# The shared expert's weights and five of its up products moved into the last heads of the first attention

## The reference, cut to what matters

```python
xn = _layernorm(x, axis=-1)
x = x + _L0_attn_ref(xn, Wq, Wk, Wv, Wo) + _L0_ffn_ref(xn, Wg, Wu, Wd, W1, W2)
# in _L0_ffn_ref, xt = xn as (4096, 256):
    h = _gelu(jnp.einsum('td,edf->tef', xt, Wu))      # routed experts, top 2 of 8
    moe = jnp.einsum('ted,te->td', jnp.einsum('tef,efd->ted', h, Wd), cw)
    shared = _gelu(xt @ W1) @ W2                      # W1: 256 x 512, W2: 512 x 256
    return shared + moe
```

## Time and profile before

| | |
|---|---|
| three timed runs | 1799.65, 1786.23, 1797.02 us (median 1797.02) |
| the profiled execution | 1787.63 us, of which the span from first to last instruction is 1785.9 us |
| busy in the span | PE 91%, PE weight loads 68%, DVE 48%, ACT 38%, POOL 42% |
| the chain that ended last | PE 78%, DVE 12%, nothing that the profile shows 4%, ACT 2%, POOL 2%, DMA 1% |
| mean granted clock of PE | 0.955 of 2.4 GHz |

### The profile page before, as it was taken

How to read it: one execution, slowest core, us unless ns; L and a number is a source line. 1 busy time by engine, 2 the same in 40 slices (tenths; PEclk the granted TensorE clock), 3 DMA queues, 4 the chain that set the end, 5 groups by cost and what they waited for, 6 DMA issues and landing times.

```text
span 1785.9 us, 32079 instructions
## 1 busy us (share of the span) xinstructions
PE 1624.5 (91%) x10912; PEld 1212.2 (68%) x10912; DVE 864.5 (48%) x2460; ACT 677.6 (38%) x1680; POOL 741.4 (42%) x845
## 2 busy tenths in 40 slices
PE   6888879898978999999987679998999999999997
PEld 3444434454434899999654346666899999999996
DVE  6787776676721233333164898987322122222221
ACT  4444434454551122222353234432533333333332
POOL 3122234556530255555532248886133333333332
PEclk9799989899988999999998799999999999999999
DMA  8444243345205122222532255544622222222221
GB/s 246 95 124 94 64 92 63 88 75 106 57 4 224 34 72 72 72 71 71 161 111 67 98 171 106 105 88 111 228 37 36 37 37 38 37 38 38 37 36 21
DMA packets 80027, 149.99 MB, mean 84 GB/s; under 512 B 13220, under 2 KB 61472, under 8 KB 73920
## 3 DMA queue, kind: packets, MB, share of 16 engines
q1 hardware_dynamic: 55328, 110.56, 24.1%
q0 software_dynamic: 24544, 37.38, 9.8%
HBM read 103.05 MB, written 44.45 MB: 83 GB/s over the span
## 4 chain that ended last, share of the span: by engine, by line
PE 78%; DVE 12%; issue 4%; ACT 2%; POOL 2%; DMA 1%; DVEq 0%; SPq 0%; ACTq 0%; POOLq 0%
PE PS L1458 21%; PE PS L1476 21%; PE PS L1344 5%; DVE PS L1765 4%; PE PS L1571 3%; PE PS L1423 3%; PE PS L1432 2%; PE PS L1280 2%; PE PS L1662 2%; PE PS L1308 2%; PE PS L1329 2%; PE PS L1443 2%; PE PS L1370 2%; PE PS L1290 2%; PE PS L1581 1%
## 5 line engine op out<-in xcount | busy, mean ns | idle before, releaser
L1458 PEld LDWEIGHTS PS<-arena 128*128 128x128 f32 x3408 | 399.5, 193 | 15.8 <-DVE arena L1988 4.6
L1458 PE MATMUL PS<-arena 128*128 128x128 f32 x3408 | 406.4, 276 | 3.2 <-DVE arena L1988 3.2
L1476 PE MATMUL PS<-arena 128*128 x1704 | 392.3, 379 | 0.0
L1476 PEld LDWEIGHTS PS<-arena 128*128 128x128 f32 x1704 | 311.6, 190 | 40.2 <-issue 0.2
L1988 DVE COPY arena<-PS 128x256 f32<-128x256 f32 x142 | 60.2, 424 | 414.4 <-PE PS L1443 404.0
L1765 DVE CUSTOM_DVE_ANT_0 PS<-PS,arena 128x512 f32<-128x512 f32 (+3 forms) x512 | 234.0, 523 | 31.6 <-PE PS L1308 31.3
L881 POOL DMA_INDIRECT out<-arena x71 | 111.6, 1572 | 314.0 <-ACT arena L1130 293.2
L1120 ACT ACTIVATE arena<-PS,arena 128x128 f32<-128x128 f32 x568 | 161.8, 368 | 138.0 <-PE PS L1458 137.9
L1057 ACT ACTIVATE arena<-PS 128x512 f32<-128x512 f32 (+1 forms) x256 | 167.2, 705 | 74.1 <-PE PS L1329 71.7
L821 POOL TENSOR_SCALAR_AFFINE_SELECT arena<-arena 128x256 f32<-128x256 f32 x256 | 98.2, 409 | 233.0 <-ACT arena L1057 231.8
L867 POOL DMA_INDIRECT arena<-XN,arena x142 | 141.5, 997 | 120.0 <-PE PS L1443 80.9
(11 more groups left out here) (242 smaller groups left out, 2059.7 us busy)
## 6 DMA issues: line engine op xcount, KB each, us to landing
arena<-FD SPq DMA_DIRECT2D x32, 512.0 KB
arena<-in_w SPq DMA_DIRECT2D x16, 1024.0 KB
SPL<-arena SPq DMA_DIRECT2D x32, 384.0 KB, 2.6
arena<-SPL SPq DMA_DIRECT2D x30, 384.0 KB
XN<-arena SPq DMA_DIRECT2D x16, 512.0 KB, 3.2
arena<-SUM SPq DMA_DIRECT2D x16, 512.0 KB, 4.9
arena<-SPL SPq DMA_DIRECT2D x30, 256.0 KB
arena<-SPL SPq DMA_DIRECT2D x34, 128.0 KB, 4.1
```

Source lines behind the costliest of these rows:

```text
L1458: ins = pe.matmul(o, m.now[i % 2][:, c * F + 128 * f:c * F + 128 * f + 128], m.xt[i % 2][:, 128 * c:128 * c + 128], start=(c == 0), stop=( ...
L1476: ins = pe.matmul(to, m.hT[i % len(m.hT)][:, 128 * c:128 * c + 128], m.WD[:, bass.ds(e * (nf * 256) + c * 256, 256)], start=(c == 0), stop ...
```

## The change

The tiles W1 and W2 move to the place of PT (the splits), and are loaded as soon as the last group's splits have been written out, 24 heads before the end. `hs[0]` moves into a pair of STK buffers that the last groups don't use, WD0 behind it. The bias tables are staged over WQ and WK, six heads earlier. Five up products enter plan0: (0,0) before head 120's `scoresT`, (0,1) and (0,2) before the last two `values`, (0,3) after the last `scale`, (1,0) between the two halves of the last `output`. For batch 0 each of the four has a bank of its own (0 to 3), which the scores have left. Their Gelus stand after the last head's Exp. PE and ACT no longer wait for the attention's end before the shared expert, and PE's two waits for banks stand behind it.

```diff
@@ attention_order
         if idx % 8 == 0 and 3 <= idx // 8 + 2 < NHB:
             out.append(("stack", idx // 8 + 2))
-        if idx == NH - 6:
+            if idx // 8 + 2 == NHB - 1:
+                out.append(("shared_weights",))
+        if idx == NH - 12:
             out.append(("bias_rows",))
+        if idx == NH - 8:
+            out.append(("shared_up", 0, 0))
+        if idx == NH:
+            out += [("shared_gelu", 0, fc) for fc in range(3)]
...
             gq = idx // 4 - 1
+            if gq >= 2 * NHB - 2:
+                out.append(("shared_up", 0, gq - 2 * NHB + 3))
             out.append(("values", gq // 2, gq % 2))
...
     while waiting:
         step()
+        if out[-1] == ("scale", NHB - 1, 1):
+            out += [("shared_up", 0, 3), ("shared_gelu", 0, 3)]
+        elif ("unscaleT", NHB - 1) in out[-2:] and ("shared_up", 1, 0) not in out:
+            out += [("shared_up", 1, 0), ("shared_gelu", 1, 0)]
@@ build, the tiles
-        bstage = view(stk_end - 1280, 256)
+        bstage = view(base, 256)
...
-        WD0 = view(base + 8192, 8192)
-        top[0] = LIMIT - 11776
-        W1 = view(carve(1024), 1024).rearrange("p (c n) -> p c n", c=2)
-        W2 = view(carve(1024), 1024).rearrange("p (c n) -> p c n", c=4)
-        hs = [view(carve(2048), 2048).rearrange("p (c n) -> p c n", c=4) for _ in range(2)]
+        hs_at = base + 10240
+        WD0 = view(hs_at + 2048, 8192)
+        W1 = view(pt_at, 1024).rearrange("p (c n) -> p c n", c=2)
+        W2 = view(pt_at + 1024, 1024).rearrange("p (c n) -> p c n", c=4)
+        top[0] = LIMIT - 7680
+        hs = [view(at, 2048).rearrange("p (c n) -> p c n", c=4) for at in (hs_at, carve(2048))]
@@ sync
             def bias_rows():
-                sp.wait_ge(st_made, 16 * (NHB - 1))
+                sp.wait_ge(qk_made, 2 * NHB)
...
+                elif kind == "shared_weights":
+                    for m in range(2):
+                        sp.wait_ge(spl_out[(NHB - 1) % 3][m], 16 * ((NHB - 1) // 3 + 1))
+                    sp.dma_start(W1[:, :, :], t["W1"]).then_inc(w12_in, 16)
+                    sp.dma_start(W2[:, :, :], t["W2"]).then_inc(w12_in, 16)
...
-            attention_over(sp)
-            sp.dma_start(W1[:, :, :], t["W1"]).then_inc(w12_in, 16)
-            sp.dma_start(W2[:, :, :], t["W2"]).then_inc(w12_in, 16)
-            for q in range(4):
-                sp.dma_start(WU0[:, 2048 * q:2048 * q + 2048], t["Wu"][:, 2048 * q:2048 * q + 2048]).then_inc(wu_in, 16)
             sp.wait_ge(b_cut, 5)
             sp.wait_ge(b_set, 1)
             for k in range(3):
                 sp.dma_start(B2S[8 * k:8 * k + 8, :], b3[0:8, k, :]).then_inc(b_rows, 16)
+            attention_over(sp)
+            sp.wait_ge(b_rows, 48)
+            sp.wait_ge(b1_turned, 1)
+            for q in range(4):
+                sp.dma_start(WU0[:, 2048 * q:2048 * q + 2048], t["Wu"][:, 2048 * q:2048 * q + 2048]).then_inc(wu_in, 16)
@@ scalar
+            for b in range(1, HB):
+                for fc in range(1 if b == 1 else 0, 4):
+                    shared_up(b, fc)
             attention_over(act)
-            for b in range(HB):
-                for fc in range(4):
-                    shared_up(b, fc)
@@ tensor
+            def shared_up(b, fc):
+
+                bk = fc if b == 0 else fc % 2
+                if b == 0 and fc == 0:
+                    pe.wait_ge(w12_in, 32)
+                    pe.wait_ge(s_max, 4 * NH)
+                elif b == 0 and fc == 3:
+                    pe.wait_ge(p_made, 2 * NH)
+                elif b:
+                    pe.wait_ge(sh_gelu, 4 * b + fc - 1)
...
+            for b in range(1, HB):
+                for fc in range(1 if b == 1 else 0, 4):
+                    shared_up(b, fc)
+                for i in range(4):
+                    shared_down(b - 1, i)
+            for i in range(4):
+                shared_down(HB - 1, i)
 
             pe.wait_ge(bank[un_last[0]], un_last[1] + 1)
             pe.wait_ge(bank[wo_in_bank[0]], wo_in_bank[1] + 1)
-            pe.wait_ge(w12_in, 32)
...
```

More of the change, by code:

```diff
@@ L341, in build @@
         R16 = [view(carve(16), 16) for _ in range(2)]
+        pt_at = top[0]
         PT = [view(carve(768), 768, BF16).rearrange("p (k s) -> p k s", k=3) for _ in range(2)]
@@ L354, in build @@
         WST = [view(pb0 + 512 * n, 512) for n in range(2)]
-        bstage = view(stk_end - 1280, 256)
-        b3 = view(stk_end - 1024, 3 * 128, BF16).rearrange("p (k n) -> p k n", k=3)
-        b1row = view(stk_end - 512, 128)
+        bstage = view(base, 256)
+        b3 = view(base + 256, 3 * 128, BF16).rearrange("p (k n) -> p k n", k=3)
+        b1row = view(base + 640, 128)
         tiles4 = lambda v: v.rearrange("p (i d) -> p i d", i=4)
@@ L368, in build @@
         WU0 = view(base, 8192)
-        WD0 = view(base + 8192, 8192)
-        top[0] = LIMIT - 11776
-        W1 = view(carve(1024), 1024).rearrange("p (c n) -> p c n", c=2)
-        W2 = view(carve(1024), 1024).rearrange("p (c n) -> p c n", c=4)
-        hs = [view(carve(2048), 2048).rearrange("p (c n) -> p c n", c=4) for _ in range(2)]
+        hs_at = base + 10240
+        WD0 = view(hs_at + 2048, 8192)
+        assert stk_end - 8192 == hs_at and hs_at + 2048 + 8192 <= pt_at
+        W1 = view(pt_at, 1024).rearrange("p (c n) -> p c n", c=2)
+        W2 = view(pt_at + 1024, 1024).rearrange("p (c n) -> p c n", c=4)
+        top[0] = LIMIT - 7680
+        hs = [view(at, 2048).rearrange("p (c n) -> p c n", c=4) for at in (hs_at, carve(2048))]
         moe0_at = top[0]
@@ L1070, in unscaleT @@
                 act.activation(OTT[n % 2][:, :], ps(bk, 0, 512), ACT.Copy).then_inc(bank[bk])
+            def shared_up(b, fc):
+                act.wait_ge(sh_made, 4 * b + fc + 1)
+                if b >= 2:
+                    act.wait_ge(sh_down, 4 * b - 4)
+                act.activation(hs[b % 2][:, fc, :], ps(fc if b == 0 else fc % 2, 0, 512), ACT.Gelu).then_inc(sh_gelu)
             for kind, *a in plan0:
@@ L1090, in scalar @@
                     values(*a)
+                elif kind == "shared_gelu":
+                    shared_up(*a)
                 elif kind == "unscaleT":
@@ L1095, in scalar @@
                     act.activation(RR[0].A, RR[0].A, ACT.Exp).then_inc(r_exp)
[L1097 to L1101, removed]
             def expert_up(layer, i):
@@ L1385, in slots, with shared_up @@
                 ins.then_inc(slot_turned)
+            def shared_up(b, fc):
+                bk = fc if b == 0 else fc % 2
[6 more added lines that the diff above has]
+                    pe.wait_ge(sh_gelu, 4 * b + fc - 1)
+                for c in range(2):
+                    ins = pe.matmul(ps(bk, 0, 512), W1[:, c, 128 * fc:128 * fc + 128], xnT[:, c, 512 * b:512 * b + 512], start=(c == 0), stop=(c == 1))
+                ins.then_inc(sh_made)
             for kind, *a in plan0:
@@ L1397, in tensor @@
                     project_v(*a)
+                elif kind == "shared_up":
+                    shared_up(*a)
                 elif kind == "scores":
@@ L1416, in tensor @@
                     slots(0, 5)
[L1418 to L1424, removed]
             def shared_down(b, i):
@@ L1490, in experts @@
                         expert_down(layer, j)
+            for b in range(1, HB):
[5 more added lines that the diff above has]
+                shared_down(HB - 1, i)
             pe.wait_ge(bank[un_last[0]], un_last[1] + 1)
             pe.wait_ge(bank[wo_in_bank[0]], wo_in_bank[1] + 1)
-            pe.wait_ge(w12_in, 32)
-            for b in range(HB):
-                for fc in range(4):
-                    shared_up(b, fc)
-                if b:
-                    for i in range(4):
-                        shared_down(b - 1, i)
-            for i in range(4):
-                shared_down(HB - 1, i)
             pe.wait_ge(sh_added, 4 * HB)
```

## The result

The changed kernel takes 1774.2 us (median of 11 runs, 1766.7 to 1785.1), the kernel before, beside it, 1797.3 us (11 runs, 1784.5 to 1804.1). The ratio is 0.9883, 95% interval 0.9854 to 0.9911: some 21 us, or 1.2%, faster. The profiled execution has a span of 1776.6 us. It took 1778.4 us, 4.2 above the median of its kernel, while that of before, with 1787.6, lies 9.7 under its own.

The account below looks back on a forecast made before the run. PE was taken as the bound, busy throughout the following stage, so earlier gains carry through. 17.1 us (wait and stage) plus 0.7 in the attention made 17.8, say 18; 1792.6 less 18 gave 1775 us, range 1763 to 1787.

Parts of the forecast that it names:

- The wait for W1: Before the shared expert's first up product: PE's wait for the weights' fetch goes, gaining 5.3 us.
- The stage at full clock: Shared expert behind the attention: 44.6 us become 32.8, 3.3 by clock and 8.6 by five products moved out.
- What the products cost: Last heads: five up products take 8.6 us at full clock, waits hide 5.3, so 3.3 us are added.
- bias_rows: Step moved six heads earlier: POOL's wait nearly goes, but product (0,1) stands there as long, so nothing counted.
- The clock in the last heads: Last three `values` and last `output` lose 6.8 us at 1.2 GHz; 4 come back, all 6.8 at best.
- ACT: Before the copy for `scale`: table load and three Gelus, 3.1 us, fit in 3.4; rival, ACT becomes the bound: chance 0.10.
- Wu and Wd: Expert weights' loads after the attention: Wu due at about 33 us, some 20 us of slack, cost nothing.
- From the sum to the time: Whole kernel: the mean of four times shown, 1792.6, less 18 us gives 1774.6, so 1775 us.
- What the profile after would show: Signs: no W1 wait, up products at 1.72 us, attention's end at 542 to 545, later stages as long as before.
- full price: Rival, last heads: clock falls as before, some products run at 1.2 GHz; gain 9 to 14 us, chance 0.17.
- the moved wait: Rival, head 120: W1 is not in, PE stops and the 5.3 us return; gain 12 us, chance 0.04.
- the late Wu: Rival, first expert: Wu lands over 33 us after the attention's end; 19 us lost, time 1812, chance 0.03.

Follow-up runs that it names:

- the fetch alone: The kernel after, but all twelve shared up products stay behind the attention; 1784.4 and 1786.4 us, ratio to before 0.992 both times.
- The refilled kernel: The kernel after with six up products in the attention instead of five, placed at PE's waits for ACT and DVE; 1773.2 us, ratio to before 0.988.

## Why the prediction was right, point by point

- **The wait for W1, 5.3 us.** Right. It is gone from the chain, and the stage of the fetch alone is shorter by it.
- **The stage at full clock, 44.6 to 32.8 us.** Right. From the attention's end to the first expert it took 52.8 and takes 35.5: 17.2 less (before rounding) against 17.1. The forecast took the first expert's products as unchanged; they gave 1.4 us more.
- **What the products cost, 8.6 - 5.3 = 3.3 us at full clock.** Right in the trace: 9.5 us of PE's waits became 4.2. (One of those waits, 1.82 us, is longer than the 1.72 of the product put there, so 5.2 would have been the exact count.) The refilled kernel shows the rest of the rule, a sixth product in 0.80 + 0.74 us of wait with the attention no longer for it.
- **bias_rows, nothing.** Right in the kernel after (0.1 us). Moved alone it is worth 1.3 us of wait.
- **The clock in the last heads, "I take 4 of the 6.8".** This term was too small, and its best bound too. The attention went from 38.65 to 34.16, 4.5 us less, with 3.3 us more of work: 7.8 us of clock. All of the 6.8 came back, and 1.0 more that the four rows did not hold, the short pieces between them (four products of scores 1.25 us where 0.72 is full, and the like). The prediction had (0,0) meet the fall at 508.3; no trace with the filling products shows any fall in that stretch. And the loss itself is not fixed: the second trace of before has 1.5 us more of it. Nor is it the products' place alone that moves the clock: without any product in the waits the attention took 33.2 to 40.1 us in five traces.
- **ACT.** Right. The table load lies directly behind an Exp, the Gelu 1.30 us behind its start, and ACT has 0.51 us to spare where 0.3 was worked out. By the Trainium skill (ScalarE: Activation LUTs, What ACT_TABLE_LOAD costs) a switch is 2.66 us, which would have made PE wait longer than 0.80 us before `scale`. The trace does not agree: PE waits 0.80, as before the change (0.79).
- **Wu and Wd.** Right in the result. The slack was put at 20 us and is 18: Wu is in 15.3 us after the attention's end (seen in the kernel that stages the first experts early), and the first copy is due at about 33.5.
- **From the sum to the time.** The sum was 17.8 and 21.7 us is what the stretches show, so it was 4 us too small, all by the clock in the last heads. The starting point, the mean of the four times shown, 1792.6, was 4.7 us under the median of 11 runs, 1797.3. The two errors cancel in 1775, and part of how near it came is luck. The chance of 0.60 for over 1% shows how close to that line the sum stood.
- **What the profile after would show.** All signs came but two. The attention ends at 548.1 and not at 542 to 545, because the trace is 7.7 us behind that of before at the maxima's last DMA; from there on the attention is shorter than forecast. And the later stages are not as long as before in this trace (1193.0 us against 1188.3), with the cause open.

Of the rivals, full price, ACT, the moved wait and the late Wu did not happen.

## What to carry to other kernels

A product can be moved into another phase's waits at little cost if it is put exactly where the engine waits, and if it is no longer than that wait; count the waits first, since what exceeds them is paid. On PE such filling bought back clock here as well, 7.8 us beside 5.3 us of waits, so price the rows at 1.2 GHz too. When two traces are compared, compare the stretch that the change touches, from a mark before it to a mark behind it, and then look once beyond that mark: here the spans differed by 9 us where the stretch, and the times, differ by 21, and the refilled kernel's 1.8 us were gone 6 us behind the stretch.

## What the runs showed of the hardware that was not expected

- The time of this kernel varies by some 20 us from run to run (before: 1784.5 to 1804.1), and PE's clock goes with it: in one series of 17 runs of the kernel before, the two slowest, 1809.6 and 1804.1 us, had a mean granted clock of 0.951, and the fastest, 1784.0, had 0.963. In the same program before the change the last part of the attention had a granted clock of 0.78 in one trace and 0.70 in another, and took 38.7 and 40.1 us. With the filling products six kernels in eight traces took 34.1 to 34.3 us there at a clock of 1.00.
- In that stretch of the kernel before, PE's longest single wait was 1.8 us, and its clock fell to 1.2 GHz several times. In the kernel after, with 4.2 us of waits left and the longest of them 0.80, it stayed at 2.4 GHz. What between the two decides, no run here tells.
